# Row maxima stored by another engine's queue in a decayed-attention block on one core

## The reference

```
x = x + attn(layernorm(x))
x = x + ffn(layernorm(x))

attn:  q, k, v = x W^T + b                       (per head)
       scores = (q k^T / 4) * sum_n mix[h,n] * decay[h,n] ** |i - j|
       out = softmax(scores) v Wo^T + bo
ffn:   W1, W2 rounded to -1, 0, 1 by their mean magnitude
       relu(x W1q^T + b1) W2q^T + b2
```

## Time and profile before

| what | value |
|---|---|
| median of 3 runs | 2094.12 us (2091.3 to 2095.25) |
| the profiled execution | 2092.2 us |
| its span | 2090.4 us |
| TensorE busy | 1686.1 us, 81% |
| VectorE, ScalarE, GpSimd busy | 71%, 68%, 44% |
| granted TensorE clock, mean | 0.902 |
| data moved | 299.98 MB, 144 GB/s in the mean |
| first unit's scores start | 178.67 us |
| last step's scores start | 1838.89 us |

### The profile page before, as it was taken

One profiled execution on the slowest core, in us unless ns is written; L12 is line 12 of the kernel. 1 busy time (PEld: TensorE's weight loads), 2 busy tenths in 40 slices (PEclk: granted clock), 3 DMA queues, 4 the chain that ended last, 5 costly groups with the idle time before them and its releaser, 6 DMA issues.

```text
span 2090.4 us, 31133 instructions
## 1 busy us (share of the span) xinstructions
PE 1686.1 (81%) x10834; PEld 586.6 (28%) x10834; DVE 1481.9 (71%) x2637; ACT 1421.2 (68%) x2670; POOL 914.3 (44%) x915
## 2 busy tenths in 40 slices
PE   7726969696959697887959695969597887979998
PEld 5401312121213132222312121212122222223666
DVE  5846858584848686685848584848587775867786
ACT  6434859494948586776849594948486776868665
POOL 5813627271716354453626271717254543525010
PEclk9857989898979899898979897979898998989999
DMA  6976555647374737465555647383737475563450
GB/s 210 307 216 142 138 133 138 154 114 183 99 189 105 172 102 173 111 160 130 139 126 139 139 130 164 101 191 103 178 91 177 110 163 128 129 167 92 113 153 31
DMA packets 181388, 299.98 MB, mean 144 GB/s; under 512 B 90576, under 2 KB 114000, under 8 KB 166992
## 3 DMA queue, kind: packets, MB, share of 16 engines
q1 hardware_dynamic: 179376, 297.86, 56.5%
q10 hardware_dynamic: 1856, 0.14, 0.1%
HBM read 152.18 MB, written 42.99 MB: 93 GB/s over the span
## 4 chain that ended last, share of the span: by engine, by line
PE 49%; DMA 14%; DVE 13%; issue 7%; SPq 7%; POOL 1%; ACT 1%; DVEq 0%; ACTq 0%
PE tile L1603 17%; PE ring L1618 17%; DMA q_stack<-max_rows 14%; PE ring L1572 9%; DVE masked L1365 4%; DVE unseen L1365 4%; SPq L147 3%; SPq L127 2%; PE tile L1600 2%; PE ring L1688 2%; SPq L116 1%; PE tile L1670 1%; POOL lo L216 1%; DVE max_rows L1385 1%; DVE qk L1453 1%
## 5 line engine op out<-in xcount | busy, mean ns | idle before, releaser
L1321 ACT ACTIVATE probs<-tile 128x512 f32<-128x512 f32 x2048 | 1114.4, 605 | 524.2 <-PE tile L1600 381.4
L1365 DVE CUSTOM_DVE_ANT_0 unseen<-ring,mask 128x1024 bf16<-128x1024 f32 x512 | 625.7, 1222 | 421.8 <-PE ring L1572 420.8
L1603 PE MATMUL tile<-q_stack,k_stack 98*128 98x512 f16 (+2 forms) x2560 | 639.2, 336 | 310.5 <-DMA q_stack<-max_rows 306.0
L1365 DVE CUSTOM_DVE_ANT_0 masked<-ring,mask 128x1024 f32<-128x1024 f32 x512 | 625.6, 1222 | 72.8 <-PE ring L1572 55.6
L1158 POOL COPY diag<-masked 128x128 f32<-128x128 f32 x512 | 149.2, 291 | 960.8 <-DVE part_max L1365 956.2
L1618 PE MATMUL ring<-probs,v_ones 128*32 128x512 f32 x4096 | 559.3, 618 | 0.1
L1603 PEld LDWEIGHTS tile<-q_stack,k_stack 98*128 98x128 f16 x2560 | 202.6, 99 | 926.3 <-issue 436.4
L1572 PE MATMUL ring<-k_raw,q_raw 64*128 64x512 f16 x2048 | 353.1, 394 | 55.1 <-PEq L225 31.2
L197 POOL TENSOR_TENSOR decayed<-qk,table_in 128x1024 f32<-128x1024 f32 x120 | 284.5, 2371 | 0.0
L216 POOL TENSOR_TENSOR lo<-decayed,hi 128x1024 f16<-128x1024 f32 x120 | 256.8, 2140 | 0.0
L210 ACT CAST hi<-decayed 128x512 f16<-128x512 f32 (+1 forms) x248 | 158.0, 637 | 10.4 <-DVE decayed L197 10.3
(11 more groups left out here) (151 smaller groups left out, 967.5 us busy)
## 6 DMA issues: line engine op xcount, KB each, us to landing
mask<-mask_row_scratch SPq DMA_DIRECT2D x32, 1984.0 KB, 20.9
k_stack<-hi SPq DMA_DIRECT2D x128, 256.0 KB, 6.1
q_stack<-hi SPq DMA_DIRECT2D x256, 128.0 KB, 4.0
table_in<-table_scratch SPq DMA_DIRECT2D x64, 256.0 KB, 9.4
q_raw<-raw_scratch SPq DMA_DIRECT2D x128, 128.0 KB
k_stack<-lo SPq DMA_DIRECT2D x64, 256.0 KB, 4.9
q_stack<-lo SPq DMA_DIRECT2D x128, 128.0 KB, 10.5
out_scratch<-heads_out SPq DMA_DIRECT2D x64, 256.0 KB, 5.5
```

The lines of the kernel that those rows point to most:

```text
L1321: nc.scalar.activation(probs[:, t % 4, half * 512:(half + 1) * 512], tile[:, (EXPS * o + n) % TILE_BANKS], ACT.Exp, scale=1.0 / (SCALE * S ...
L1365: nc.vector.tensor_tensor_reduce(out=masked[:, b % 2] if diagonal else unseen[:], in0=pair, in1=factor, scale=1.0, scalar=-3.0e38, op0=ALU ...
L1603: last = nc.tensor.matmul(out, k_stack[h][:, level, kb * P:(kb + 1) * P], q_stack[h][:, half, level, first - half * HALF:first - half * HA ...
```

## The change

It has three parts.

1. The row maxima are issued by ScalarE. It does so in slot 6 of a unit (`TURN_SLOT + 1`), behind that slot's four exponentials and its cast, on its own DMA queue. SyncE no longer waits for the turns. So that raw rows and mask are not overwritten while they are read, SyncE now waits for VectorE to have taken the last block of the head: slot 3's for head 0 (`BLOCKS - 1 - LEAD`), slot 19's for head 1.
2. `load_levels`, the stack loads of the first head, moves from the token part to the start of the attention part. The waits on the token part's stores move there too: on SyncE behind these loads and ahead of the first max pass load, on ScalarE ahead of the constants. Tiles are allocated in another order, so that the tiles with late stores (`raw_out`, `q_out`, `k_out`, `v_out`) lie under `q_stack1` and `k_stack1`, which are first written behind those waits.
3. At the start of the attention part `v_ones` is loaded ahead of the second half's `q_stack`.

```diff
+    def wait_stores(self, eng):
+        for u in range(2):
+            eng.wait_ge(self.stored[u], GROUPS // 2 * self.STORES * QUADS)
+            eng.wait_ge(self.raw_stored[u], GROUPS // 2 * 2 * QUADS)
+
+    def load_levels(self, sp, x):
+        sp.wait_ge(self.lo_ready, 4 * x + 4)
+        self.load_part(sp, self.k_stack, 0, 1, self.k_in[x], 2 * x, 2, 0, SEQ)
+        self.load_part(sp, self.q_stack, 0, 0, self.q_in[x], 2 * x, 2, 0, HALF)
...
@@ token part, SyncE @@
-                if g == GROUPS - 2:
-                    load_levels(0)
                 store_qk(g)
...
             store_raw(GROUPS - 1)
-            load_levels(1)
-            for u in range(2):
-                sp.wait_ge(stored[u], GROUPS // 2 * STORES * QUADS)
-                sp.wait_ge(raw_stored[u], GROUPS // 2 * 2 * QUADS)
             sp.wait_ge(later_in, 2 * QUADS)
...
@@ attention part, SyncE @@
-            def store_max_rows(h, half, taken):
-
-                sp.wait_ge(ring_free, taken)
-                sp.dma_start(q_stack[h][STACK:STACK + MAXROWS, half],
-                             max_rows[:]).then_inc(rows_in, QUADS)
-
...
+            for x in range(2):
+                builder.load_levels(sp, x)
+            builder.wait_stores(sp)
             load_max_pass(1, 0)
+            load_v(0, 0)
             for x in range(2):
                 load_q(0, 1, x)
-            load_v(0, 0)
             builder.load(sp, 1)
-            store_max_rows(0, 0, turn_taken(TURN_SLOT - UNIT_SLOTS, True, 0))
...
-                store_max_rows(0, 1, turn_taken(TURN_SLOT, more, o))
...
                 if more:
+                    sp.wait_ge(ring_free, items_done(BLOCKS - 1 - LEAD, o))
                     load_max_pass(0, i + 1)
...
-                store_max_rows(1, 0, turn_taken(UNIT_SLOTS + TURN_SLOT, more, o))
...
-                store_max_rows(1, 1, turn_taken(2 * UNIT_SLOTS + TURN_SLOT, more, o))
...
                 if more:
+                    sp.wait_ge(ring_free, items_done(SLOTS - 1 - LEAD, o))
                     load_max_pass(1, i + 1)
...
-                if more:
-                    store_max_rows(0, 0, turn_taken(3 * UNIT_SLOTS + TURN_SLOT, more, o))
...
@@ attention part, ScalarE @@
             act.wait_ge(unit_ready, 1)
+            builder.wait_stores(act)
...
+            def store_max_rows(h, half, taken):
+
+                act.wait_ge(ring_free, taken)
+                act.dma_start(q_stack[h][STACK:STACK + MAXROWS, half], max_rows[:]).then_inc(rows_in, QUADS)
+
             nc.scalar.activation(warm[:], ident[:, 0:1], ACT.Exp)
             repeat_max(0, 1)
+            store_max_rows(0, 0, turn_taken(TURN_SLOT - UNIT_SLOTS, True, 0))
...
                         cast(*cast_slot[s], i + 1)
+                    if s % UNIT_SLOTS == TURN_SLOT + 1 and (more or s + UNIT_SLOTS < SLOTS):
+                        u = s // UNIT_SLOTS + 1
+                        store_max_rows(u // 2 % 2, u % 2, turn_taken(s - 1, more, o))
```

More of the change, by code:

```diff
@@ L104, in __init__ @@
         self.raw_in, self.mask_in = sem("raw_in0"), sem("mask_in0")
+        self.stored = [sem(f"stored{u}") for u in range(2)]
+        self.raw_stored = [sem(f"raw_stored{u}") for u in range(2)]
         self.k_in, self.q_in = ([sem(f"{n}_in0_{x}") for x in range(2)] for n in ("k", "q"))
@@ L147, in load_part @@
             sp.dma_start(dst, part[row:row + ROWS, level:level + count, first:first + columns]).then_inc(done, QUADS)
+    STORES = 3
+    def wait_stores(self, eng):
[6 more added lines that the diff above has]
+        self.load_part(sp, self.q_stack, 0, 0, self.q_in[x], 2 * x, 2, 0, HALF)
     def loaded(self, builds):
@@ L230, in sem @@
             return ctx.enter_context(nc.semaphore(name))
+        raw_out = sb("raw_out", [P, 2, 2, 2, 2, GROUP], F16)
+        q_out = sb("q_out", [P, 2, 2, GROUP])
+        k_out = sb("k_out", [P, 2, 2, GROUP])
+        v_out = sb("v_out", [P, 2, TILES, EMBED])
         wn = sb("wn", [P, 4, EC, EMBED])
@@ L249, in token_block @@
         row_out = sb("row_out", [P, 2, 2 * P])
-        raw_out = sb("raw_out", [P, 2, 2, 2, 2, GROUP], F16)
         x = sb("x_tokens", [P, XBUFS, TILES, EMBED])
@@ L253, in token_block @@
         xt_lo = sb("xt_lo", [P, 2, EC, GROUP], F16)
-        q_out = sb("q_out", [P, 2, 2, GROUP])
-        k_out = sb("k_out", [P, 2, 2, GROUP])
-        v_out = sb("v_out", [P, 2, TILES, EMBED])
         stats = sb("stats", [P, 2, TILES, 6])
@@ L275, in token_block @@
         raw_hi, raw_ready = sem("raw_hi"), sem("raw_ready")
-        raw_stored = [sem(f"raw_stored{u}") for u in range(2)]
+        raw_stored = builder.raw_stored
         rows_in = [sem(f"first_rows{g}") for g in range(4)]
         x_loaded = [sem(f"x_loaded{u}") for u in range(XBUFS)]
-        stored = [sem(f"stored{u}") for u in range(2)]
+        stored = builder.stored
         sqrt_in, sqrt_out, shift_ready, hat_done = sem("sqrt_in"), sem("sqrt_out"), sem("shift_ready"), sem("hat_done")
@@ L283, in token_block @@
                                                       sem("q_taken"), sem("k_taken"))
-        STORES = 3
+        STORES = builder.STORES
         HALF_GROUPS = GROUPS // BATCH
@@ L351, in load_first_raw @@
                 load_raw_head(sp, scr["raw"], builder.q_raw, builder.k_raw, 0, 0, builder.raw_in)
[L353 to L356, removed]
             load_x(0)
@@ L822, in attention_and_ffn_block @@
         k_stack = [builder.k_stack, sb("k_stack1", [STACK + MAXROWS, DEPTH, SEQ], F16)]
+        probs = sb("probs", [P, 4, HALF])
         mask = [builder.mask, sb("mask1", [P, MASK])]
@@ L825, in attention_and_ffn_block @@
         k_raw = [builder.k_raw, sb("k_raw1", [P, 2, GROUP], F16)]
-        probs = sb("probs", [P, 4, HALF])
         diag = [sb(f"diag{h}", [P, BLOCKS, P]) for h in range(2)]
```

## The result

| | before | changed |
|---|---|---|
| median, us (4 runs each) | 2092.71 (2091.2 to 2095.25) | 2182.57 (2178.45 to 2183.84) |
| ratio, 95% interval | | 1.0425 [1.0406, 1.0443] |
| span of the profiled execution | 2090.4 | 2176.7 |
| TensorE busy, us | 1686.1 | 1749.5 |
| mean granted clock | 0.902 | 0.895 |

The forecast was 1927, range 1855 to 2020: the time lies outside it, and on the other side of no change.

A forecast was written before the change was run, and what follows sets the result against it. It took the bound to be TensorE's wait for row maxima at step changes, behind two loaded DMA engines. 2092.2 less 143 (stalls) and 24 (first step) gave 1925, with 1.9 for the median 1927 us; range 1855 to 2020.

The forecast's parts named there:

- The rows leave SyncE's queue; the stacks leave 11.3 us: Step change: with the rows on ScalarE's queue, the stack loads alone would leave 11.3 of the 20.2 us wait.
- The raw loads go 5.5 us earlier: Second head's raw loads start 5.5 us earlier, stack loads follow: step change 5.8 us, 6.8 with the rows sharing the engines.
- The rows' landing, 6.6 us: Slots 6 and 22: rows land 6.6 us after issue beside raw loads, less 3.2 us allowance: a stall of 3.4 us.
- The `b_col` row: Profile row of a transfer on ScalarE's queue beside SyncE's full one, read as 65 packets in 9 us, 0.14 us each.
- The upper bound of 7 us: Slots 6 and 22: largest stall allowed for the rows, from twice the time beside larger neighbours.
- Slot 22's stall comes off the step change: The 3.4 us stall at slot 22 comes off the step change's 6.8 us, as the two loaded engines go on meanwhile.
- The clock stays in the sum as it is: TensorE's restart: a stall of 6.8 us also pays the slow restart, so the sum has no separate clock term.
- ScalarE's issue costs nothing: Row issues on ScalarE: charged nothing, as a 0.38 us issue ran while activations were still executing.
- the prediction's own sign of being wrong: ScalarE's row issues: the prediction called itself wrong if they last over 1 us.
- Rival C: Slower: ScalarE's issue stuck at a full queue, 8 us more at slot 6 and the step change; 2166 us, chance 0.06.
- The first step, 24 us: Kernel start: attention part starts near 123 instead of 136, first rows land at 154.3 against 178.67: 24 us less.
- the wait for `q_stack<-max_rows`: Sign of success in TensorE's list of waits: this one falls from 306 to under 100 us.

The follow-up runs named there:

- act_early: The kernel before, with row maxima issued by ScalarE after slots 5, 13, 21 and 29 and raw loads at their old places; 1997.79 us.
- act_only: The kernel before, with row maxima issued by ScalarE as in the change and raw loads still at their old places, after slots 5 and 21; 2168.80 us.
- raw_after_rows: The change, with SyncE holding raw loads and mask until the row maxima of slots 6 and 22 have landed; 2168.40 us.
- mask_after_rows: The change, with only the mask held on SyncE until the row maxima of slots 6 and 22 have landed; 2105.19 us.
- spread_after: The change, with each raw load split in two to run on sixteen DMA engines instead of two, same bytes; 1909.44 us.
- mask_ahead: The change, with the mask issued first and the raw loads held until the row maxima of slots 6 and 22 have landed; 2044.15 us.

## Why the prediction was wrong

1. **The rows leave SyncE's queue; the stacks leave 11.3 us.** Right in kind. Where the stacks end the wait (act_early) it is 13.6 us in the mean, 2.3 more than read. A part of that was in the rows of before: TensorE waits for both groups of stack loads, and the prediction took the landing of the first `q_stack<-lo` (1037.30 + 20.5). The second was issued at 1039.23 and landed after 19.8 us, 8.3 us before the restart, not 9.5, and 7.6 in the mean, not 8.9: 12.6 us would be left, not 11.3. In the change itself the stacks limit nothing: the same load, issued at 1093.82, lands after 2.6 us, 4 us before TensorE stops.
2. **The raw loads go 5.5 us earlier.** They do (behind `v_ones`, 1055.39 and 1056.09), and it is worth something: in act_only, where they go out at the old places, the step change stops for 9.6 us in the mean instead of 6.3, and in raw_after_rows, where they go later still, for 16 to 21. But they and the mask are ahead of the rows of slot 22. The prediction counted the gain in full and the price with 3.4 us.
3. **The rows' landing, 6.6 us: the step that failed.** It was 1 us until the first packet plus 33 x 0.14 to 0.2 (4.6 to 6.6). The second term was right in size: about 4.1 us beside raw loads alone, 0.13 a packet, and 5.0 to 5.5 with the mask. The first was about 4 us beside raw loads, and 4 to 6 with the mask in flight; that puts about 8.2 and 10.6 us in place of 6.6, and a stall of 5.2 to 6.4 and of 7.1 to 8.7 in place of 3.4. The 1 us came from a row with an idle queue, used for a full one. The `b_col` row had the right size in it: of its packets, issued at 105.30, 910 moved by 109.5 and none of the pair's 130 before that, so the pair's first came 4.2 us after the issue. The prediction read it as a steady pace from 109 and dropped these 4 us. And the mask of 1984 KB, issued 1.2 us ahead of the rows, had no term at all. The upper bound of 7 us was too low as well, as it doubled only the part that was right.
4. **Slot 22's stall comes off the step change.** False. The step change (6.3 us in the mean, 6.8 forecast: the size by luck) is not ended by the stacks but by the rows' own landing from slot 30, +4.4/+5.2 and +6.4/+9.2 in two steps, behind `qk` and tables. A stop at unit 3 gives these nothing, as their issue moves with it: with a stop of 7.9, 5.5 or 0 us there (the change, mask_after_rows, spread_after) the step change takes 6.3, 6.7 and 6.9. So a step loses 21.8 us (327.6 / 15), not 3.4 + 6.8.
5. **The clock stays in the sum as it is.** False: three short stops pay the slow restart three times. It is 63 of the 253 us between forecast and profile; the stalls are 178 (327.6 less 150), the first step 8. Of the 178, the landing (step 3) makes 136 at units 1 and 3 (119.6 + 118.1 - 30 x 3.4), and the give-back that did not come (step 4) 48 (14 x 3.4).
6. **ScalarE's issue costs nothing.** Right. 64 issues, 0.53 us in the median and 1.15 at most (the first, 0.15 more than the prediction's own sign of being wrong allowed), while activations ran. One of 0.55 us, at 187.37, even lies wholly inside an issue of SyncE of 8.54 us (181.81). Rival C, the one case on the slow side, named 2166 us by a mechanism that did not occur; that 2182.57 is near it speaks for nothing.
7. **The first step, 24 us.** It was 16.4: the start came at 125.00 and TensorE wanted the rows at 155.1, about as forecast (123, 153), but they were issued at 149.6 and took 12.7 us, not 6.6: step 3 again.

The prediction set aside the Trainium skill's rule ("DMA: Bandwidth & Descriptors", section "Issuing engines are not separate DMA queues": issuing from several engines saves only the time to issue) by the row of `b_col`, a transfer already under way. With 4 us without a packet, and one packet of SyncE's for each of the rows' behind that (72 to 66), the rule was nearer than the prediction's reading of the row. At slot 21 of act_early and slot 22 of mask_ahead nothing was in the way (first packet after 1.2 us), so these do not test it.

Of the prediction's own signs one was met by name only (the wait for `q_stack<-max_rows` fell to 97 us while "issue" took 237.7), and one spoke at once: TensorE waits 8 us at slot 8, not some 3.

What stays open: why a transfer on its own queue moves nothing for about 4 us on two engines that work on another's, and then alternates. The runs give the size and what it depends on, not the mechanism.

## What to carry to other kernels

Moving a small urgent transfer to another engine's queue does not take it out of the DMA engines that it shares: ask what was handed to those engines in the microseconds before its new issue, the large transfers on all sixteen too, and price the wait until its first packet apart from its passage. One queue had kept the rows ahead of the raw loads; two queues left it to a race, decided by 2.7 us here, and in spread_after by 0.02. When a DMA share reads 0.13 with one kind of transfer in flight, spread that transfer first: here it was worth 10% alone and 17% with the change and rows issued early.

## What the runs showed of the hardware

- A queue's new transfer beside another queue's backlog on the same two engines: no packet for 3.9 to 4.8 us (mask_after_rows, 3.9 at 1025.16), then one for one (66 to 72 in 4.6 us). With the mask in flight 4.0 to 6.2 us (the change).
- The order of issue decides, even by 0.02 us: first packet after 3.9 us with the mask of 1984 KB issued just ahead, after 1.4 us with it 0.6 us behind (spread_after).
- DMA issues on ScalarE ran beside its own activations (1064.64 within the activation of 1062.94, 2.29 us); none of 64 was longer than 1.15 us. One lies inside an issue of SyncE of 8.54 us (181.81).
- A wait for a DMA can stand in the list as "issue" (237.7 us here); the queue's packets name it.
- Stops of 7 to 9 us bring the granted clock from 1.00 to 0.50 as one of 20 us does, so a stall split in parts is dearer: TensorE's busy time, for the same 10834 matmuls, is 1686 us with one stop a step (before, mask_ahead), 1720 with two (raw_after_rows) and 1740 to 1750 with three (act_only, mask_after_rows, the change).
